# Attention of an attention-and-experts layer: outputs in pairs of steps, reciprocals through DRAM, another order of additions

## The reference

```python
x  = L0_attn_x                                 # (4, 2048, 512), float32
xn = layernorm(x)
q = (xn @ Wq).reshape(B, S, 4, 4, 32)          # 4 groups of 4 heads, head size 32
k = (xn @ Wk).reshape(B, S, 4, 32); v = (xn @ Wv).reshape(B, S, 4, 32)
scores = where(causal, -big, q k^T * 32**-0.5)
attn = softmax(scores) @ v                     # the part that is changed
out = x + (attn @ Wo) + moe(xn)                # moe: 32 experts, 6 of them per token, and a shared one
```

## Time and profile before

| | us |
|---|---|
| median of 3 runs (lowest to highest) | 3667.69 (3661.32 to 3669.6) |
| profiled execution | 3666.97 |
| its span in the trace, granted TensorE clock 0.992 | 3665.2 |
| `stage_b` on PE, first score to last output matmul | 1427 to 3483 |

### The profile page before, as it was taken

How to read it: one execution, slowest core, us unless ns; L and a number is a source line. 1 busy time by engine, 2 the same in 40 slices (tenths; PEclk the granted TensorE clock), 3 DMA queues, 4 the chain that set the end, 5 groups by cost and what they waited for, 6 DMA issues and landing times. The chain is left out here.

```text
span 3665.2 us, 56522 instructions
## 1 busy us (share of the span) xinstructions
PE 3555.3 (97%) x19856; PEld 2212.8 (60%) x19856; DVE 2368.1 (65%) x5390; ACT 1631.2 (45%) x3347; POOL 2083.0 (57%) x1604
## 2 busy tenths in 40 slices
PE   7999999999997999999999999999999999999899
PEld 5888888888874555555555555555555555544287
DVE  6455554554543445787787778778777877875344
ACT  3232222222321113666565566656566665656611
POOL 0333323323342223877787787778778777877800
PEclk9999999999998999999999999999999999999999
DMA  5333333232338994102211210221121022110087
GB/s 174 101 109 100 100 109 100 100 123 92 110 106 254 291 311 123 44 19 56 53 34 34 53 46 19 56 53 34 35 53 46 20 56 53 34 46 22 6 298 243
DMA packets 228173, 340.55 MB, mean 93 GB/s; under 512 B 65088, under 2 KB 75968, under 8 KB 227968
## 3 DMA queue, kind: packets, MB, share of 16 engines
q1 hardware_dynamic: 197232, 307.77, 27.6%
q0 software_dynamic: 17920, 12.82, 1.7%
q10 hardware_dynamic: 12816, 17.33, 1.3%
HBM read 217.15 MB, written 120.35 MB: 92 GB/s over the span
## 5 line engine op out<-in xcount | busy, mean ns | idle before, releaser
L1376 ACT ACTIVATE prb<-sps 128x512 f32<-128x512 f32 (+3 forms) x2560 | 1187.8, 539 | 758.0 <-PE sps L1481 725.1
L1399 DVE TENSOR_REDUCE mx<-mps 128x1 f32<-128x512 f32 x1440 | 939.5, 681 | 162.1 <-PE mps L1463 162.1
L1311 POOL TENSOR_TENSOR rows<-rows,prb 128x1024 f32<-128x1024 f32 x384 | 908.0, 2387 | 0.0
L396 POOL DMA_INDIRECT tab_s<-pay,slot x384 | 377.6, 983 | 733.9 <-DVE tokf L694 482.7
L1402 DVE CUSTOM_DVE_ANT_0 mps<-mps,bias 128x256 f32<-128x256 f32 (+1 forms) x960 | 489.1, 522 | 211.8 <-PE mps L1463 211.6
L1495 PE MATMUL ops<-prb,vst 128*32 128x512 f32 (+3 forms) x5120 | 600.4, 541 | 9.4 <-POOL prb L1296 9.0
L1305 POOL TENSOR_TENSOR rows<-prb 128x1024 f32<-128x1024 f32 x192 | 454.3, 2386 | 153.0 <-ACT prb L1376 153.0
L1463 PE MATMUL mps<-x_lo,w_lo 96*128 96x512 f32 (+2 forms) x1280 | 488.4, 388 | 8.8 <-DVE mx L1399 3.3
L1481 PE MATMUL sps<-w_lo,x_lo 97*128 97x512 f32 (+2 forms) x1280 | 477.0, 393 | 17.4 <-ACT prb L1376 17.4
L1481 PE MATMUL sps<-w_hi,x_hi 97*128 97x512 f32 (+2 forms) x1280 | 482.6, 389 | 9.7 <-ACT prb L1376 8.0
L751 PE MATMUL acc<-x_hi,w_hi 128*128 128x512 f32 x1088 | 429.8, 395 | 6.5 <-DVE qk_lo L596 6.5
(11 more groups left out here) (175 smaller groups left out, 4173.8 us busy)
## 6 DMA issues: line engine op xcount, KB each, us to landing
wgu<-in_e_gu SPq DMA_DIRECT2D x24, 1408.0 KB, 6.8
rows<-in_x SPq DMA_DIRECT2D x16, 1024.0 KB
xn_s<-rows SPq DMA_DIRECT2D x16, 1024.0 KB, 5.1
y_sb<-in_x SPq DMA_DIRECT2D x16, 1024.0 KB
q_hi_s<-qk_hi SPq DMA_DIRECT2D x16, 1024.0 KB
q_lo_s<-qk_lo SPq DMA_DIRECT2D x16, 1024.0 KB
base<-y_sb SPq DMA_DIRECT2D x16, 1024.0 KB
w_hi<-q_hi_s SPq DMA_DIRECT2D x64, 256.0 KB, 4.2
```

Of the source, the lines that this page charges most:

```text
L396: nc.gpsimd.indirect_dma_start(t["tab"], bass.IndirectOffsetOnAxis(ap=slot[:, i, k:k + 1], axis=0), pay[:, i, k, :], None, bounds_check=E ...
L1311: nc.gpsimd.tensor_tensor(acc4, acc4, prb[:, (2 * n + pr) % RP], ALU.add).then_inc(add_done, 1)
L1376: nc.scalar.activation(prb[:, (2 * k + h // 2) % RP, h % 2, q0:CH], sps[:, (GROUP * k + h) % R, q0:CH], ACT.Exp, scale=SCALE).then_inc(exp ...
L1399: V.tensor_reduce(mx[:, h * NKT + qt, j:j + 1], mps[:, n % R, 0:wr], AX.X, ALU.max).then_inc(mred_done, 1)
```

## The change

In `group` of `block.tensor` the loop goes over pairs of steps: the eight scores of steps k and k+1, with the pieces of both among them (a piece now ahead of its score, and pieces beyond the eighth at the very start), then `sum_of_four`, then the output matmuls of steps k-2 and k-1. The planner no longer gives fewer pieces to the steps in which DVE inverts. DVE no longer inverts 128x512: the denominators of a block, 4 heads x 512 columns that stand 32 times over in `den`, are written to DRAM once (4 DMAs of 2 KB), read back as 128x16, inverted in one instruction (step last + 7), written back, and read into `rden` with each head spread over 32 partitions (4 DMAs). SP issues them, in `denominators` and `reciprocals`, between its stores. POOL normalizes at last + 10, after the selections of its step. Of the four whose next step is on the diagonal POOL makes the last four additions later: the third at f+4 and f+5 and the fourth at f+6 and f+7, one a step and behind the selections. ACT takes over the turned maxima one step earlier. For the last block of all the four reciprocals stay, in `stage_c`.

```diff
+        EL = GROUP * CH // P
+        dsm = two("dsm", [P, EL])
+        rsm = two("rsm", [P, EL])
...
+        INVERTED, SCALED = LAG + 5, LAG + 8
         diag = [n for n, (j, kt, r) in enumerate(steps) if r >= 0]
         lasts = [n for n, (j, kt, r) in enumerate(steps) if r == 3]
 
+        def third(f, pr):
+
+            return f + 4 + pr if f + 4 in diag else f + 3
+
         def fourth(f, pr):
 
-            return f + 4 + (pr if f + 4 in diag else 0)
+            return f + 6 + pr if f + 4 in diag else f + 4
...
-        for k in range(M1):
-            if any(k - LAG - 1 - part in lasts for part in range(NT)) or LAG <= k < LAG + NT:
-                work[k] -= 400
...
+            def denominators(n):
+
+                q = n % JC % 2
+                sp.wait_ge(den_done, n + 2)
+                for h in range(GROUP):
+                    sp.dma_start(t["den"][q, h:h + 1], den[q][HD * h:HD * h + 1, :]).then_inc(den_out, 16)
+                sp.wait_ge(den_out, 16 * GROUP * (n + 1))
+                sp.dma_start(dsm[q][:], t["den"][q].rearrange("h (c e) -> (h c) e", e=EL)).then_inc(dsm_in, 16)
+
+            def reciprocals(n):
+
+                q = n % JC % 2
+                sp.wait_ge(rsm_done, n + 1)
+                sp.dma_start(t["rec"][q].rearrange("h (c e) -> (h c) e", e=EL), rsm[q][:]).then_inc(rec_out, 16)
+                sp.wait_ge(rec_out, 16 * n + 16)
+                for h in range(GROUP):
+                    sp.dma_start(rden[q][HD * h:HD * (h + 1), :],
+                                 t["rec"][q, h:h + 1].to_broadcast([HD, CH])).then_inc(rden_in, 16)
+
+            def blocks(i, p):
+
+                n = (2 * i + p) * JC
+                if n:
+                    denominators(n - 1)
+                    reciprocals(n - 1)
+                denominators(n)
+                if n:
+                    store((n - 1) // JC // 2, (n - 1) // JC % 2, JC - 1)
+                reciprocals(n)
+                store(i, p, 0)
+                for j in range(1, JC - 1):
+                    denominators(n + j)
+                    reciprocals(n + j)
+                    store(i, p, j)
...
-                    for j in range(JC - 1):
-                        store(i, p, j)
+                    blocks(i, p)
                     for c in range(JC):
...
-                pool.wait_ge(rden_done, NT * (bg * JC + j + 1))
+                pool.wait_ge(rden_in, 16 * GROUP * (bg * JC + j + 1))
...
-                    if k - LAG - NT - 1 in lasts:
-                        normalize(bg, lasts.index(k - LAG - NT - 1))
-                    if prev and k == LAG + NT:
-                        normalize(bg - 1, JC - 1)
...
+                    if k - SCALED in lasts:
+                        normalize(bg, lasts.index(k - SCALED))
+                    if prev and k == SCALED - 1:
+                        normalize(bg - 1, JC - 1)
...
-                            elif k == f + 3 or k == fourth(f, pr):
-                                n = f + 2 if k == f + 3 else f + 3
+                            elif k == third(f, pr) or k == fourth(f, pr):
+                                n = f + 2 if k == third(f, pr) else f + 3
...
-                    if nxt and k == MFIN + 2:
+                    if nxt and k == MFIN + 1:
...
-            def invert(bg, j, part):
-
-                if part == 0:
-                    dve.wait_ge(den_done, bg * JC + j + 2)
-                cols = slice(part * P, (part + 1) * P)
-                V.reciprocal(rden[j % 2][:, cols], den[j % 2][:, cols]).then_inc(rden_done, 1)
+            def invert(bg, j):
+
+                dve.wait_ge(dsm_in, 16 * (bg * JC + j + 1))
+                V.reciprocal(rsm[j % 2][:], dsm[j % 2][:]).then_inc(rsm_done, 1)
...
-                    for part in range(NT):
-                        if k - LAG - 1 - part in lasts:
-                            invert(bg, lasts.index(k - LAG - 1 - part), part)
-                        if prev and k == LAG + part:
-                            invert(bg - 1, JC - 1, part)
+                    if k - INVERTED in lasts:
+                        invert(bg, lasts.index(k - INVERTED))
+                    if prev and k == INVERTED - 1:
+                        invert(bg - 1, JC - 1)
...
-                for k in range(NK):
-                    todo = list(quota(k)) if nxt else []
-
-                    for h in range(GROUP):
-                        scores(bg, p, k, h)
-                        for n in todo[h:h + 1]:
+                for k in range(0, NK, 2):
+                    todo = list(quota(k)) + list(quota(k + 1)) if nxt else []
+                    extra = max(len(todo) - 2 * GROUP, 0)
+                    for n in todo[:extra]:
+                        piece(bg + 1, 1 - p, n)
+                    for u in range(2 * GROUP):
+                        for n in todo[extra + u:extra + u + 1]:
                             piece(bg + 1, 1 - p, n)
+                        scores(bg, p, k + u // GROUP, u % GROUP)
                     for gi, f in enumerate(fours):
-                        if k == f + DUE:
+                        if k + 1 == f + DUE:
                             sum_of_four(bg, gi)
-                        if prev and k + NK == f + DUE:
+                        if prev and k + 1 + NK == f + DUE:
                             sum_of_four(bg - 1, gi)
-                    if k >= LAG:
-                        output(bg, p, k - LAG)
-                    elif prev:
-                        output(bg - 1, 1 - p, NK + k - LAG)
-                    for n in todo[GROUP:]:
-                        piece(bg + 1, 1 - p, n)
-                    if nxt and k == MFIN:
+                    for n in (k, k + 1):
+                        if n >= LAG:
+                            output(bg, p, n - LAG)
+                        elif prev:
+                            output(bg - 1, 1 - p, NK + n - LAG)
+                    if nxt and k + 1 == MFIN:
...
-            pool.wait_ge(rden_done, NT * (LAST + 1))
+            pool.wait_ge(rden_done, NT)
...
+            "den": dram("den_s", [2, GROUP, CH], F32), "rec": dram("rec_s", [2, GROUP, CH], F32),
```

More of the change, by code:

```diff
@@ L1185, in stage_b @@
             att[n] for n in ("qk_in", "v_in", "c_in", "c_done", "m_done", "mred_done"))
-        att_out, att_done, rden_done, den_done = (car[n] for n in ("att_out", "att_done", "rden_done", "den_done"))
+        att_out, att_done, den_done = (car[n] for n in ("att_out", "att_done", "den_done"))
+        den_out = sem("den_out")
+        dsm_in = sem("dsm_in")
+        rsm_done = sem("rsm_done")
+        rec_out = sem("rec_out")
+        rden_in = sem("rden_in")
         s_done = sem("s_done")
@@ L1262, in _ @@
                     load_v(sp, t, att, i + 1, p)
-                    store(i, p, JC - 1)
             sp.dma_start(wo[:], t["w_o"].rearrange("(k p) n -> p k n", p=P)).then_inc(car["wo_in"], 16)
-            for j in range(JC):
-                store(BG // 2 - 1, 0, j)
+            blocks(BG // 2 - 1, 0)
             sp.wait_ge(s_done, (BG - 1) * NU)
@@ L1269, in _ @@
                          ).then_inc(car["a_ld0"], 16)
-            for j in range(JC - 1):
-                store(BG // 2 - 1, 1, j)
+            blocks(BG // 2 - 1, 1)
         @block.gpsimd
```

## The result

| | before | after |
|---|---|---|
| median, us (runs) | 3668.64 (4) | 3745.11 (4) |
| span of the profiled execution | 3665.2 | 3743.3 |
| mean granted TensorE clock | 0.992 | 0.984 |

The ratio is 1.0215 (95% interval 1.02 to 1.0231): slower by about 76 us. The forecast was slower by 34, within 3662 to 3722; the sign was right, the size less than half of what came.

The account below looks back on a forecast made before the run. The prediction took PE to set the pace in the attention stage. 15 groups at +2.65 us (39.8) less 6 for the last gave +33.8; 3667.0 + 33.8 + 0.7 = 3701.5 us, range 3662 to 3722.

Parts of the forecast that it names:

- Part 1, excursions: PE's changes of shape around output bursts: 20 of 40 a group go, 0.30 us each, 6.0 us a group gained.
- Part 1, the ring: Three maxima buffers between PE and DVE: in pairs, PE's waits for DVE grow from 3.7 to 11.1 us a group.
- Moved as well ... Cost 0: Turn and ACT's copy of the maxima one step earlier: the last pair of 5.5 us hides the row's write; cost 0.
- Group 15 (-6): Last group of the attention stage, which has no pieces: 6 us shorter, between -12 and +3.
- POOL's part: Last group: with selections first, most of PE's 9 us of waits for them goes; -7 us.
- the plain cost of the pairs: Last group: a pair takes 5.43 us against 2 x 2.63, as scores wait for exponentials; +1 us.
- Part 2, the chain through DRAM: Reciprocals' way through DRAM: landings of 2.0 to 2.7 us, covered by 5.8 and 2.6 us; cost 0.
- The crowded loads of Q and K: SP's loads, behind the chain, come three or four steps later; first needed at the next group; cost 0.
- worth next to nothing: Freeing DVE of reciprocals: 1.3 us a group in the old order, next to nothing in pairs, where they fill DVE's idle time.
- The rival of a late DRAM chain: Landings over 4 us with SP's loads queued hold normalization, selections and additions: 2 us a block, 128 us, 3830; chance 0.05.
- The rival in which subtractions and additions hold each other up: Last group: VectorE's subtractions and the moved POOL additions exclude each other, the 6 us are given back, 3707; chance 0.08.

Follow-up runs that it names:

- e6: The changed kernel with DVE's reductions of full pieces over 256 of their 512 columns (half of those keys left out of the maxima); 3667.7 us.
- e7: The kernel before with DVE's reductions of full pieces over 256 of their 512 columns, as the control; 3638.7 us.
- e10: e9 with ACT copying the turned maxima behind the last exponentials of a group; 3767.4 us.
- e1: The kernel before with only PE's loop over pairs of steps and the earlier copy of the maxima; reciprocals, POOL's order and planner as before; 3795.1 us.
- e3: The kernel before with only POOL's later additions, one a step and behind the selections; 3662.0 us.
- e8: The changed kernel with an unused matmul ahead of each score in the last pair of each group and in all of group 15; 3722.7 us.
- e4: The changed kernel with PE's old loop over single steps and the copy of the maxima at its old step; 3693.2 us.
- e5: e4 with SP's loads of Q and K at the steps of the kernel before; 3651.0 us.
- e9: The changed kernel with SP's loads of Q and K at the steps of the kernel before; 3742.5 us.

## Why the prediction was wrong, point by point

**Part 1, excursions (6.0 us a group): right in mechanism, not isolated in size.** There are 20 excursions in place of 40, and two bursts run 1.85 us as one. No run isolates their worth: e6 against e7 shows the change winning 1.3 us in steps 2 to 37, and about 0.5 of that is part 2's. The 6.0 rests on the pairs coming out as worked out, next.

**Part 1, the ring (+7.4): right, pair by pair.** The 18 pairs from step 2 to step 37 of group 5 took 118.44 us; the same working gives 118.21, and no pair is off by more than 0.10:

| pair from step | 2 | 4 | 10 | 22 | 28 | 34 |
|---|---|---|---|---|---|---|
| measured, us | 7.44 | 5.42 | 7.21 | 7.72 | 6.53 | 6.27 |
| worked out | 7.34 | 5.40 | 7.13 | 7.78 | 6.57 | 6.30 |

e6 and e7 show that DVE's pitch is the cause, and measure 4.4 of the 7.4 us. (The rule of the Trainium skill quoted there, TensorEngine Tiling (Array Packing), PSUM Bottleneck, agrees with the traces in this much, that the emptying of PSUM is what PE waits for, 740 times where it was 277.)

**"Moved as well ... Cost 0" failed.** This was the mis-sized term: the earlier copy of the maxima. I checked that its transfer is covered and not what stands behind it on ACT. The last pair was worked out as 5.54 us and took 7.83. The steps between are each measured: 5.5 with the copy behind the exponentials (e10, without its wait for the row), 6.23 with the early copy and no fall of the clock (e1), 7.83 with the fall. So of the 2.3 us, 0.7 is the copy and its issue ahead of exponentials for which PE waits, and 1.6 the clock, which was no term at all. 15 groups by 2.3 are 34 of the 44 us that the forecast missed (the rest of a group came out 0.25 us lower than forecast, which takes 4 of them back).

**Group 15 (-6): failed.** POOL's part was about right (e3: 5.7 shorter; I had 7), so was the plain cost of the pairs: with full clock e8 takes 126.9 against 125.3 for e4, +1.6 where I had +1. But in the paired order the clock came down to a mean of 0.90, which costs 7.6 us by e8, so that the group came out 4.4 longer. That is 10 of the 44. Nowhere in the prediction is the clock a term, though the trace of before had it at 0.93 to 0.94 in group 15.

**Part 2, the chain through DRAM: right where it was costed.** Landings take 1.4 to 2.0 us, and no compute engine waits for it in groups 1 to 14. Two statements around it failed, both hidden in this result. The crowded loads of Q and K: I looked at who needs them, not at who shares the DMA engines with them; without the earlier copy they cost 42 us (e4 against e5). The other is that the reciprocals are "worth next to nothing" in the paired order because they would fall in DVE's idle time behind a burst: they stand between the two steps' reductions, and together with the planner's uneven shares that go with them they are worth 50 us there (e1 against after, whose group 15 is no shorter).

**The rival of a late DRAM chain** had the wrong link (landings of the chain) but the right neighbourhood. The rival in which subtractions and additions hold each other up gave nothing back: after, the first subtraction takes 12.4 us and not 7.3, but all eight together take 21.0 and not 21.7, and from the last output matmul to the end are 182.0 us against 182.1.

The remaining 3.5 us lie ahead of the attention stage in unchanged code; in the other runs that stage starts between 1424 and 1431, so this is the spread of executions.

What stays open: why the clock falls at the end of all 15 groups after and in e9, but at the end of only two in e1, where PE was busy 2.08 of 3.09 us before the burst and waited as long, and at changing places in e8. The price of a fall is measured, its condition is not.

## What to carry to other kernels

Merging the outputs of two steps halves the changes of shape, but it also doubles the run of work that a ring of three buffers must carry: compare the pitch of the producer within the run with the pitch of the consumer, not their shares of the time. When an instruction is moved, cost what is queued behind it on its engine, and when a transfer is moved, cost whose transfer it then meets. A wait of a microsecond in a thin stretch of matmuls can be paid twice, the second time by the clock in the work behind it; look at the granted clock of such stretches in every run, since the same stretch may pass without a fall in a kernel that differs elsewhere.

## What the runs showed of the hardware

- The granted clock fell after a stretch in which PE was busy 2.27 of 3.29 us with no wait over 1.02, and eight 512-column output matmuls then took 1.94 us in place of 1.06. It did not fall in 13 of 15 groups of e1 after the same matmuls and the same wait (2.08 of 3.09 us busy). A fall at the end of a group cost 1.6 us.
- Unused matmuls in the last pairs and in group 15 made the kernel 22 us faster (e8), 7.6 of them in group 15, where the mean clock went from 0.90 to 1.00.
- A 32 KB transfer on ACT's queue landed in 2.6 to 2.7 us with the 64 to 256 KB loads spaced out, in 4.9 with 1 MB of them issued right ahead and beside it (e10), in 5.2 to 6.1 when issued 2 to 3 us behind 2.9 MB of them, and in 7.4 to 8.1 when issued 0 to 0.6 us behind those (e6).
- Small transfers through DRAM landed in 1.6 us (8 KB, 64 bytes a partition, read) and 1.4 (written), four at a time with 2 KB a partition in 2.0.
- A reciprocal of 128x128 on DVE takes 0.94 us.
